# Attention values as stationary operand, softmax sums from the exponential's accumulator: one change to a fused attention and feed-forward kernel

## The reference, cut to what matters

```python
def _div_clamp_fp8(x, scale):
    y = jnp.clip(x.astype(jnp.float32) / scale, -FP8_MAX, FP8_MAX)
    y = y.astype(jnp.bfloat16).astype(jnp.float32)
    return _fp8_roundtrip(y)
def _gqa(q, k, v):
    scale = 1.0 / np.sqrt(q.shape[-1])
    scores = jnp.einsum('bsghd,btgd->bghst', q, k) * scale
    p = jax.nn.softmax(scores, axis=-1)
    return jnp.einsum('bghst,btgd->bsghd', p, v)
...
core = _gqa(q, k, v).reshape(b, s, nh * d)
xout = _gqa(qx, kx, vx).reshape(b, s, nh * d)
cat = jnp.concatenate([core, xout], axis=-1)
catq = _div_clamp_fp8(cat, proj_smooth)
return jnp.einsum('bsi,oi->bso', catq, wproj) * (proj_in_scale * proj_w_scale)
```

## Time and profile before

| | |
|---|---|
| median of 3 runs | 1736.24 us (1735.25 to 1736.79) |
| the profiled execution | 1738.57 us, span 1736.7 us from its first to its last instruction |
| PE busy | 1632.1 us, 94% of the span |
| DVE, ACT, POOL busy | 1410.2 us, 1359.8 us, 1089.6 us |
| granted TensorE clock | 0.992 of full speed over the span |

### The profile page before, as it was taken

The page is one execution under the profiler, slowest core; times in us unless marked ns, Lnnn a source line. Parts: engine busy times, 40 slices in busy tenths (PEclk is TensorE's granted clock), DMA queues, the critical chain, the costliest instruction groups (busy, mean ns, idle before and its releaser), DMA issues.

```text
span 1736.7 us, 43799 instructions
## 1 busy us (share of the span) xinstructions
PE 1632.1 (94%) x15491; PEld 1228.0 (71%) x15776; DVE 1410.2 (81%) x3228; ACT 1359.8 (78%) x2908; POOL 1089.6 (63%) x1031
## 2 busy tenths in 40 slices
PE   1569999999999999999999999999999899999999
PEld 1447778888888888888888888888888544444444
DVE  8999999999999999999999999998779763323232
ACT  6978999999999999999999999999999622222221
POOL 1357777777787777777777777778777613121211
PEclk9969999999999999999999999999999999999999
DMA  5947788887888888788878887888999980303000
GB/s 177 223 111 127 140 154 144 148 153 147 148 149 156 147 145 152 147 148 146 151 147 149 148 159 147 145 140 151 188 187 187 196 244 22 138 8 142 4 24 25
DMA packets 663603, 241.45 MB, mean 139 GB/s; under 512 B 619488, under 2 KB 636000, under 8 KB 662880
## 3 DMA queue, kind: packets, MB, share of 16 engines
q1 hardware_dynamic: 662096, 230.20, 68.1%
q0 software_dynamic: 1296, 8.52, 2.4%
HBM read 75.15 MB, written 29.51 MB: 60 GB/s over the span
## 4 chain that ended last, share of the span: by engine, by line
PE 71%; DVE 9%; ACT 7%; issue 5%; POOL 4%; SPq 3%; DMA 2%; DVEq 0%; ACTq 0%; POOLq 0%
PE ps_pj L673 21%; PE ps_s L739 6%; PE ps_o L722 5%; PE ps_o L724 5%; PE ps_o L723 5%; PE ps_s L742 5%; PE ps_s L680 4%; PE ps_qt L692 4%; POOL local L1131 2%; PE ps_s L738 2%; PE ps_pj L811 2%; PE ps_s L825 2%; PE ps_o L811 2%; PE ps_pj L812 2%; PE ps_o L812 2%
## 5 line engine op out<-in xcount | busy, mean ns | idle before, releaser
L1131 POOL TENSOR_TENSOR local<-local 128x512 bf16<-128x512 f32 x512 | 597.1, 1166 | 296.3 <-ACT local L1035 296.0
L673 PE MATMUL ps_pj<-wide 128*128 128x256 bf16 (+1 forms) x5544 | 582.7, 254 | 4.8 <-DVE wide L1214 4.0
L673 PEld LDWEIGHTS ps_pj<-wide 128*128 128x128 bf16 x5544 | 470.1, 98 | 115.0 <-DVE wide L1214 4.4
L1032 ACT ACTIVATE local<-ps_s,neg_max 128x512 f32<-128x512 f32 x512 | 391.8, 765 | 43.7 <-DVE neg_max L1429 41.6
L1035 ACT ACTIVATE local<-ps_s,neg_max 128x512 bf16<-128x512 f32 x512 | 394.0, 770 | 0.0
L722 PE MATMUL ps_o<-v_hi,local 128*128 128x129 bf16 x2048 | 375.5, 221 | 5.7 <-DVE local L1437 3.2
L724 PE MATMUL ps_o<-v_hi,local 128*128 128x129 bf16 x2048 | 375.2, 219 | 0.0
L723 PE MATMUL ps_o<-local 128*128 128x128 bf16 x2048 | 375.1, 218 | 0.0
L1429 DVE TENSOR_REDUCE neg_max<-ps_s 128x1 f32<-128x512 f32 x512 | 344.7, 673 | 22.8 <-PE ps_s L742 22.7
L941 ACT ACTIVATE local<-ps_pj,head_rstd 128x128 f32<-128x128 f32 x756 | 242.0, 448 | 41.8 <-issue 41.7
L1106 POOL TENSOR_TENSOR head_rstd<-sq_sum,minus_half 128x3 f32<-128x3 f32 x256 | 223.4, 873 | 16.4 <-DVE sq_sum L1321 16.4
(11 more groups left out here) (133 smaller groups left out, 2623.5 us busy)
## 6 DMA issues: line engine op xcount, KB each, us to landing
quantised_heads<-local SPq DMA_DIRECT2D x128, 128.0 KB, 2.4
w_raw<-w_group SPq DMA_DIRECT2D x56, 256.0 KB, 3.2
wide<-quantised_heads SPq DMA_DIRECT2D x3, 4096.0 KB, 13.1
local<-local SPq DMA_TRANSPOSE x640, 3.2
wide<-packed_weights SPq DMA_DIRECT2D x32, 256.0 KB, 3.2
wide<-x SPq DMA_DIRECT2D x6, 1024.0 KB, 12.0
packed_weights<-w_proj POOLq DMA_DIRECT2D x4, 1024.0 KB, 15.2
wide<-quantised_heads SPq DMA_DIRECT2D x16, 256.0 KB, 3.4
```

Of the source, the lines that this page charges most:

```text
L673: last = mm(dst[:, at:at + n], lhs, w_at(par, part, c, cross * 512 + at, n), start=(k == 0), stop=(k == len(terms) - 1))
L1032: a(p_exp[:, u % 2], ps_s[u % 2][:], ACT.Exp, bias=neg_max[:, u % 4:u % 4 + 1])
L1131: tt_(pp[:, u % PP_BUFS, 1], p_exp[:, u % 2], pp[:, u % PP_BUFS, 0], ALU.subtract)\
```

## The change

It does four things.

1. The value product is turned round: `v_hi` and `v_lo` are the stationary operand, the transposed probabilities of two units (256 queries) the moving one. The output has channels on partitions and queries along the row, so the heads need no DMA transpose and are stored as they are. The product of a pair is made in two halves, in two slots (`values(u, start, end)`), and a head has one bank.
2. The softmax sums come from the f32 exponential by `accum_out`. Since they stand one query on each partition and are now needed along the row, DVE inverts a head's four columns at once, SP writes them to DRAM (`SUM_OUT_LAG`) and reads them back to all partitions (`SUM_IN_LAG`). DVE scales a whole head in one instruction of 512 columns, ahead of the rounding.
3. `QUANT_LAG` goes from 6 to 8 and `QUANT_END_LAG` from 9 to 11.
4. In the groups, the copy of the value part into `v_hi` moves from ACT to DVE.

```diff
-        MAX_LAG, EXP_LAG, LO_LAG, TURN_LAG = 1, 1, 1, 3
-        PV_LAG, Y_LAG, HEAD_LAG, STORE_LAG = 5, 6, 10, 12
+        MAX_LAG, EXP_LAG, LO_LAG, TURN_LAG = 1, 1, 1, 3
+        PV_LAG, STORE_LAG = 5, 12
+        SUM_LAG, SUM_OUT_LAG, SUM_IN_LAG = 2, 3, 5
-        QUANT_LAG, QUANT_END_LAG = 6, 9
+        QUANT_LAG, QUANT_END_LAG = 8, 11
...
 # SP
                         if not first or u >= PT_BUFS:
-                            sp.wait_ge(pv_done, SLOTS * g + u - PT_BUFS + 1)
+                            sp.wait_ge(pv_done, SLOTS // 2 * g + (u - PT_BUFS) // 2 + 1)
...
+                    for H in head_at(slot, SUM_OUT_LAG, first):
+                        n = GROUP_HEADS * g + H
+                        sp.wait_ge(rsum_done, n + 1)
+                        sp.dma_start(sums_dram[n].rearrange("(p t) -> p t", t=TT), r_inv[:, H % 2]).then_inc(sums_out[H % 2], 16)
+                    for H in head_at(slot, SUM_IN_LAG, first):
+                        n = GROUP_HEADS * g + H
+                        sp.wait_ge(sums_out[H % 2], 16 * (n // 2 + 1))
+                        sp.wait_ge(y_done, n - 1 + HEAD_FREE)
+                        sp.dma_start(inv_sums[:, H % 2], sums_dram[n].partition_broadcast(P)).then_inc(sums_in[H % 2], 16)
...
 # PE
+            def values(u, start, end):
+
+                b, cross = u // UNITS, u // TT % HEADS // HPG
+                at = (u - 1) % TT * P
+                acc = ps_o[u // TT % 2][:, at:at + 2 * P]
+                pair = slice((u - 1) % PT_BUFS, (u - 1) % PT_BUFS + 2)
+                for tc in range(start, end):
+                    vh, vl = v_hi[:, b % 2, cross, tc], v_lo[:, b % 2, cross, tc]
+                    ph, pl = pt[:, pair, tc], pt[:, pair, TT + tc]
+                    mm(acc, vh, ph, start=(tc == 0), stop=False)
+                    mm(acc, vl, ph, start=False, stop=False)
+                    last = mm(acc, vh, pl, start=False, stop=(tc == TT - 1))
+                return last
...
+                    for u in unit_at(slot, PV_LAG + 1, first):
+                        if u % 2 == 1:
+                            values(u, TT // 2, TT).then_inc(pv_done, 1)
                     for u in unit_at(slot, PV_LAG, first):
+                        if u % 2 == 1:
+                            for i in (u - 1, u):
+                                pe.wait_ge(pt_landed[i % PT_BUFS], 16 * SLOTS // PT_BUFS * g + 16 * (i // PT_BUFS + 1))
+                            pe.wait_ge(y_done, GROUP_HEADS * g + u // TT - 1 + HEAD_FREE)
+                            values(u, 0, TT // 2)
...
 # ACT
-                        v_part(b, i, t)
...
-                        a(p_exp[:, u % 2], ps_s[u % 2][:], ACT.Exp, bias=neg_max[:, u % 4:u % 4 + 1])
+                        a(p_exp[:, u % 2], ps_s[u % 2][:], ACT.Exp, bias=neg_max[:, u % 4:u % 4 + 1],
+                          accum_out=r_sum[:, H % 2, qt:qt + 1])
...
 # DVE
-                    for u in unit_at(slot, Y_LAG, first):
-                        dve.wait_ge(pv_done, SLOTS * g + u + 1)
-                        v.reciprocal(r_sum[:, u % 4:u % 4 + 1], ps_o[u % 2][:, D:D + 1]).then_inc(rsum_done, 1)
...
+                    for H in head_at(slot, SUM_LAG, first):
+                        n = GROUP_HEADS * g + H
+                        dve.wait_ge(exp_done, TT * (n + 1))
+                        if n >= 2:
+                            dve.wait_ge(sums_out[H % 2], 16 * (n // 2))
+                        v.reciprocal(r_inv[:, H % 2], r_sum[:, H % 2]).then_inc(rsum_done, 1)
...
                     for H in head_at(slot, QUANT_LAG, first):
+                        dve.wait_ge(pv_done, 2 * (n + 1))
+                        dve.wait_ge(sums_in[H % 2], 16 * (n // 2 + 1))
+                        v.scalar_tensor_tensor(y[:, H % 2].rearrange("p (t q) -> p t q", q=P),
+                                               ps_o[H % 2].rearrange("p (t q) -> p t q", q=P), smooth_of(g, H),
+                                               inv_sums[:, H % 2].rearrange("p (q t) -> p t q", t=TT), ALU.mult, ALU.mult)\
+                            .then_inc(y_done, 1)
...
                     for k in tile_at(slot, VAR_LAG, first, last):
+                        dve.wait_ge(sq_done, t + 1)
+                        v.tensor_copy(v_hi[:, b % 2, i // TT, i % TT], tile_bank(i, t)[:, 3 * D:4 * D]).then_inc(vhi_done, 1)
```

More of the change, by code:

```diff
@@ L76, in block_kernel @@
     packed = nc.dram_tensor("packed_weights", (P, (G * HEADS + HC) * DM + CH * 2 * HID), BF16, kind="Internal").ap()
[L77 removed]
+    sums_dram = nc.dram_tensor("inverse_sums", (G * B * HEADS, P * TT), F32, kind="Internal").ap()
     stack = ExitStack()
@@ L280, in block_kernel @@
         rsum_done = sem("rsum_done")
+        sums_out = [sem(f"sums_out{i}") for i in range(2)]
+        sums_in = [sem(f"sums_in{i}") for i in range(2)]
         plo_done = sem("plo_done")
         pt_landed = [sem(f"pt_landed{i}") for i in range(PT_BUFS)]
-        turned = [sem(f"turned{i}") for i in range(2)]
         pv_done = sem("pv_done")
@@ L439, in quad_place, with smooth_of @@
             return (q // 2 + 1) % 2, q % 2
-        def smooth_rows_of(group_index, head):
-            return rsmooth[:, bass.ds((group_index % 2) * (HEADS * D) + head * D, D)]
+        def smooth_of(g, H):
+            at = (g + H // GROUP_HEADS) * HEADS + H % HEADS
+            return inv_smooth[:, at:at + 1]
         def tile_bank(i, t):
@@ L581, in group @@
                         load_next_heads(slot - NEXT_HEADS)
-                    if slot == SMOOTH_SLOT and not last:
-                        sp.wait_ge(y_done, SLOTS * g + UNIT_FREE)
-                        rows = smooth_dram[bass.ds(g + 1, 1)].rearrange("o n -> (o n)").partition_broadcast(P)
-                        sp.dma_start(rsmooth[:, bass.ds(((g + 1) % 2) * (HEADS * D), HEADS * D)], rows).then_inc(smooth_in, 16)
-                    for H in head_at(slot, HEAD_LAG, first):
-                        sp.wait_ge(heads_done, GROUP_HEADS * g + H + 1)
-                        sp.sem_inc(waited_sp, 1)
-                        if not first or H >= HEADS:
-                            sp.wait_ge(heads_stored, 16 * (GROUP_HEADS * g + H - HEADS + 1 + FREE))
-                            sp.sem_inc(waited_sp, 1)
-                        sp.dma_start_transpose(heads_t[:, H % HEADS].rearrange("p (q s) -> p q s", s=P), heads_n[:, H % 2])\
-                            .then_inc(turned[H % 2], 16)
-                    for H in head_at(slot, STORE_LAG, first):
-                        sp.wait_ge(turned[H % 2], 16 * GROUP_HEADS // 2 * g + 16 * (H // 2 + 1))
+                    for H in head_at(slot, SUM_OUT_LAG, first):
[7 more added lines that the diff above has]
+                        sp.dma_start(inv_sums[:, H % 2], sums_dram[n].partition_broadcast(P)).then_inc(sums_in[H % 2], 16)
+                    for H in head_at(slot, STORE_LAG, first):
+                        sp.wait_ge(heads_done, GROUP_HEADS * g + H + 1)
                         sp.wait_ge(heads_stored, 16 * (GROUP_HEADS * g + H + FREE))
@@ L930, in v_part @@
             def v_part(b, i, t):
-                a(v_hi[:, b % 2, i // TT, i % TT, 0:D], tile_bank(i, t)[:, 3 * D:4 * D], ACT.Copy).then_inc(vhi_done, 1)
+                a(v_hi[:, b % 2, i // TT, i % TT], tile_bank(i, t)[:, 3 * D:4 * D], ACT.Copy).then_inc(vhi_done, 1)
             def head_norm(i, t, turns):
@@ L1031, in group @@
                             act.wait_ge(plo_done, SLOTS * g + u - 1)
-                        a(p_exp[:, u % 2], ps_s[u % 2][:], ACT.Exp, bias=neg_max[:, u % 4:u % 4 + 1])
+                        H, qt = u // TT, u % TT
+                        if qt == 0 and (not first or H >= 2):
+                            act.wait_ge(rsum_done, GROUP_HEADS * g + H - 1)
+                        a(p_exp[:, u % 2], ps_s[u % 2][:], ACT.Exp, bias=neg_max[:, u % 4:u % 4 + 1],
+                          accum_out=r_sum[:, H % 2, qt:qt + 1])
                         if not first or u >= PP_BUFS:
@@ L1155, in _ @@
             v.reciprocal(rscale, c_("in_scale", 0, SETS * CH)).then_inc(ones_set, 1)
-            v.reciprocal(inv_smooth[:], c_("smooth", 0, G * HEADS)).then_inc(smooth_inverted, 1)
+            v.reciprocal(inv_smooth[:], c_("smooth", 0, G * HEADS))
             v.tensor_tensor(pscale[:], c_("proj_in"), c_("proj_w"), ALU.mult)
```

64 lines of the change are left out of this document (18 added, 46 removed).

## The result

The changed kernel takes 1911.6 us, the median of four runs (1910.54 to 1913.38); the kernel before took 1735.74 us on the same chip (1733.53 to 1736.79). The ratio is 1.1017 (95% interval 1.1003 to 1.1030): slower by 176 us, where the prediction had 60 us and a range up to 1848.

The account below looks back on a forecast made before the run. It took PE as the bound, DVE and ACT close behind. Groups 1 to 6 at -1.6 + 10.5 = +8.9 us each (+53), first group +4, last +1, drain +2 made +60: 1796 us, range 1753 to 1848.

Parts of the forecast that it names:

- a: On ACT: the extra time of each f32 exponential for its accumulator output; 0.12 us taken, 0 to 0.31 possible.
- lower of the prediction's two formulas: On PE in slots 3, 7 and 11: standing for late maxima, 3.9 + 12a us a group at the least.
- Per head one scaling of 512 columns comes. ... I take 0.60.: On DVE, once per head: the new scaling instruction, taken as 0.60 us, with up to 1.2 us named.
- the weight pieces: On DVE: weight scaling sharing slots with the moved rounding, counted as 0.76 us in slot 3 and 0.52 in slot 7.
- the prediction's upper formula: On ACT: idle during DVE's stretches with little slack to recover, a loss of 12 + 48a us a group.
- PE's saving: Value product on PE: twelve matmuls of 256 columns a pair take 1.31 us instead of 1.36, -1.6 us a group.
- the rival of the unhidden weight loads: On PE: halving the weight loads saves 0.63 us a pair, 161 us in all, giving 1575 us; 1 in 100.
- The accumulator: On ACT: 0.12 us on each of 64 exponentials a group; as rival bound at 0.31, 1856 us, 9 in 100.
- The copy: On DVE, per tile: copying the value part out of PSUM, 0.20 us (0 to 0.3), 6.4 us a group.
- The DMAs: On SP: broadcast hidden, transposes cost nothing in groups 1 to 6, 3 us in the last; rival wait 1786 us, 2 in 100.
- The other stretches of the program: Outside groups 1 to 6: first group +4 us, last group +1, drain +2.
- The bursts are absorbed: Rival: maxima on DVE stay early enough, PE remains the bound and its 13 us come out; 1725 us, 12 in 100.

Follow-up runs that it names:

- e5: The kernel before with only the change's lags (QUANT_LAG 8, QUANT_END_LAG 11; head's transpose and store two slots later): 1783.81 us, ratio 1.0280.
- e6: The changed kernel with GpSimd's subtraction computing only 32 of 512 columns for all but the first units: 1832.06 us, ratio 1.0568.
- e1: The changed kernel with the rounding moved back to slots 1 mod 4 (QUANT_LAG 10, QUANT_END_LAG 13), store two slots later: 1749.37 us, ratio 1.0071.
- e7: e1 with the two DMA transposes of a pair of units issued together, the odd one a slot earlier: 1748.36 us, ratio 1.0074.
- e12: e7 without the accumulator output, the softmax sums a constant 1: 1735.19 us, ratio 1.0002.
- e2: The changed kernel with the head's scaling reading the inverse sums without a stride, so in another query order: 1869.95 us, ratio 1.0769.

## Why the prediction was right or wrong

The prediction's rule can be checked as it stands. It measured a maximum's lateness M from the start of the last score matmul, and had PE stand by M + 2.03 + a - 4.79 for slot 11 (a limit of 2.76 - a), with limits of 2.34 and 1.90, each less a, for slots 3 and 7. For slot 15 it only says that an M of 2.05 is in time; the two PE slots behind it are as long as those behind slot 3 (2.6 and 2.2 us), so 2.34 less a is taken for it. Medians over units 128 to 439, worked out from the starts in each trace (the maximum stands at the start of the next slot):

| M of the maximum behind slot | 3 | 7 | 11 | 15 | stall by the rule, us a group | group less a PE that never waits |
|---|---|---|---|---|---|---|
| forecast | 2.54 | 2.38 | 3.05 | 2.05 | 5.3 at the least, 10.5 taken | |
| before | 0.49 | 0.42 | 1.53 | 0.42 | 0 | 0 (158.8) |
| changed kernel | 3.84 | 3.76 | 4.12 | 3.58 | 25.3 | 28.0 (185.0 - 157.0) |
| e5, lags alone | 2.78 | 2.70 | 3.03 | 2.43 | 6.4 | 7.4 (166.2 - 158.8) |
| e6, short subtraction | 2.55 | 3.05 | 2.59 | 4.31 | 14.4 | 16.3 (173.3 - 157.0) |
| e1, rounding moved | 1.82 | 1.77 | 2.20 | 1.44 | 0 | 2.5 (159.5 - 157.0) |

(a is 0.09, in e5 0. 157.0 is four times 39.25, the sum of the smallest distances that e7's traces show for each of 16 slots. For the changed kernel: 1.59 + 1.95 + 1.45 + 1.33 = 6.32 in 16 slots.) The lower of the prediction's two formulas, fed with the measured M, comes out 1 to 3 us a group under the measured stall. In e1 it gives nothing, and the 2.5 there are another thing: e7 takes 0.3 of them away (the transposes), e12 1.9 more (the accumulator). So the rule held, and what failed is what was put into it.

- **Direction and mechanism: right.** Slots 3, 7, 11 and 15, the exponential as releaser, ACT's wait for the maximum. e1 and e5 show the place of the rounding as the cause, from both sides.
- **The step that failed: "Per head one scaling of 512 columns comes. ... I take 0.60."** It is 1.16 from start to start. The text named the stride, the f32 operand and 1.2 us, and then took the low end because the nearest row was 0.67. The dear end did not even enter the range, whose two formulas both have 0.60 in them. Four slots of 16 grew by 0.56 us for it. e2 shows it as a cause: 0.39 us off the scaling, 42 us off the time.
- **The second size: the weight pieces "from start to start I count 0.76, 0.52"** and 1.21. Behind the new lags they are 1.51 (three pieces, 715.63 to 717.14), 1.24 (two, 727.41 to 728.65) and 1.84. I took the durations of before as the price of the instructions; they were the price beside that kernel's GpSimd. In the changed kernel 72 of 168 scaling pieces have no subtraction beside them and take 0.335 us each, the other 96 take 1.07, every one of them. Before it was 72 and 96 again, but only 48 of the 96 took over 1 us and the mean was 0.765. e6 shows it as a cause: 80 us. With the dearer scaling it turned the sum round: DVE's work, which the prediction had falling by 3.4 us a group, rose from 149.3 to 160.9 us (busy time, mean of groups 1 to 6).
- **A third term, left out: DVE's wait for ACT.** The prediction took slot 14 as 2.05 us; it is 3.73 (slots 2 and 6: 3.38 and 3.73 against 3.05 and 3.13), as DVE stands up to 1.57 us for the squares. Without that wait M behind slot 15 would be 0.42 + 2.05 + 4.65 - 5.22 = 1.90, in time, and not 3.58. By the rule that is 1.33 us in 16 slots, some 5 us a group; this is an estimate, and no run takes that wait alone away. The prediction's own M of 2.05 there doesn't follow from its sizes either: 0.42 + 2.05 + 4.24 - 5.22 is 1.49. Its sum was not touched by that, as both are in time.
- With the first two, the stretches of slots 11, 15, 3 and 7 are 5.41, 4.65, 5.07 and 4.81 us against 4.25, 4.24, 3.87 and 3.63. Put into the prediction's upper formula they give (19.9 - 9.4 - 2.6) x 4 = 32 us a group, so the two ends 25.3 and 32 hold the measured 28.0. With 0.60 and the old pieces they were 5.3 and 17.8.
- **PE's saving: right.** 0.109 us for each 256-column matmul; a group without waits is 157.0 to 157.3 us against 158.8, so 1.5 to 1.8 less (forecast 1.6). That also settles the rival of the unhidden weight loads.
- **The accumulator: right**, 0.09 where 0.12 was taken. As a bound of its own it shows only in e7. **The copy: right**, 0.19 (697.88 to 698.07 in the changed kernel) for 0.20. **The DMAs: right**, transposes landed in

```profile
DMA to landing us min/median/max: 3.0/3.1/4.9
```

  and PE waited for none of them in groups 1 to 6.
- **The other stretches of the program: too low.** Group 0 +14.2 against +4 (DVE is the bound there, and its busy time rose from 164.6 to 175.6 us where a fall of 3.4 was counted; with e1's places it is 165.6, and group 0 takes 172.9 us), behind group 6 +5.6 against +1, drain +4.1 against +2. Only the first is explained.
- **"The bursts are absorbed" needed two slots under 7.1 us**; they were 8.4 to 8.9, so this rival never had a chance at the true sizes.
- **What was luck:** slot 10, forecast 3.60 and measured 3.52, came right although its largest part, the cast, is held up by GpSimd as well (1.53 us here, 0.68 in e6); the sum took over the 1.62 us of before, which happened to have nearly the same hold-up.

## What to carry to other kernels

Before work is moved into a slot, add up that slot as one stretch between two hand-overs, and ask how late the hand-over then is against the moment at which the other engine needs it: the same rounding cost nothing in one place, 48 us beside other work, and 162 us beside work that had just grown. A duration read from a trace is that of the instruction and of what ran beside it on the engine that shares its ports; moving it changes both. And where a new operand has a layout that no row of the trace shows, the dear end belongs into the sum, or at least into the range, before the change is made.
